# Laying out both members of 28 key pairs with ScalarE, so that GpSimd multiplies them in place with two instructions a step

## The reference

```python
sim = k @ q_i                                   # one token i, one head
_, top_idx = jax.lax.top_k(masked(sim), 8)
for comb in COMBS:                              # 8 single keys, then 28 pairs
    idx = concat(i, top_idx[comb])
    K, V = k[idx], v[idx]
    gram = jnp.einsum('cnd,cmd->cnm', K, K)     # dot products of all members
    log_det = jnp.log(where(valid, det(gram), 1.0) + 1e-06)
    score = log_det / (s + 1)
    w = softmax(K @ q_i / HS ** 0.5)
    out_s = jnp.einsum('cn,cnd->cd', w, V)
probs = softmax(scores)
y = probs @ outs
```

## Time and profile before

| | before |
|---|---|
| median of 3 runs (lowest to highest) | 6936.29 us (6931.03 to 6949.35) |
| the profiled execution: its time, its span | 6937.07 us, 6935.4 us |
| busy in the span: PE, DVE, POOL, ACT | 5118.2, 4327.0, 3276.0, 2100.8 us |
| attention phase, a stretch of 2840 us: busy PE, DVE, POOL, ACT | 2373.11, 2538.28, 1990.13, 993.06 us |

### The profile page before, as it was taken

How to read it: one execution, slowest core, us unless ns; L and a number is a source line. 1 busy time by engine, 2 the same in 40 slices (tenths; PEclk the granted TensorE clock), 3 DMA queues, 4 the chain that set the end, 5 groups by cost and what they waited for, 6 DMA issues and landing times. The chain is left out here.

```text
span 6935.4 us, 140450 instructions
## 1 busy us (share of the span) xinstructions
PE 5118.2 (74%) x45364; PEld 3716.5 (54%) x45365; DVE 4327.0 (62%) x9002; ACT 2100.8 (30%) x6098; POOL 3276.0 (47%) x4341
## 2 busy tenths in 40 slices
PE   6776766978888888888888888443980997169990
PEld 2333333765555555556555665342860776169990
DVE  5777775227888898898999999722654233212223
ACT  3343333223333333333333333222210332223330
POOL 1222222115666776777776767425236000554447
PEclk8677776996666666666666666556995997579995
DMA  4000000002222222222222222202222002111113
GB/s 138 5 7 5 7 3 6 0 5 71 74 74 70 75 72 72 73 75 71 74 72 72 75 72 75 67 26 73 75 72 68 0 0 60 52 50 46 46 42 109
DMA packets 170739, 369.46 MB, mean 53 GB/s; under 512 B 35650, under 2 KB 100939, under 8 KB 169140
## 3 DMA queue, kind: packets, MB, share of 16 engines
q1 hardware_dynamic: 136404, 283.77, 12.2%
q0 software_dynamic: 33792, 78.69, 3.6%
HBM read 286.86 MB, written 75.50 MB: 52 GB/s over the span
## 5 line engine op out<-in xcount | busy, mean ns | idle before, releaser
L2334 POOL TENSOR_TENSOR l2a_prod<-l2a_keys 128x64 f32<-128x64 f32 (+1 forms) x2304 | 1115.6, 514 | 817.2 <-ACT l2a_norms L2224 808.2
L2679 PE MATMUL l2a_g<-l2a_feat,l2a_onehot 128*128 128x33 bf16 x27648 | 894.1, 187 | 29.9 <-issue 24.8
L2679 PEld LDWEIGHTS l2a_g<-l2a_feat,l2a_onehot 128*128 128x128 bf16 x27648 | 835.8, 103 | 89.5 <-issue 61.1
L2648 PE MATMUL l2a_s<-l2a_qkT 32*128 32x128 f32 (+1 forms) x1536 | 653.6, 518 | 48.3 <-issue 48.3
L1734 POOL TENSOR_TENSOR l_hc<-l_hs,l_bc 128x512 f32<-128x512 f32 x192 | 243.0, 1266 | 803.2 <-DVE l_hs L1808 799.7
L2554 DVE TENSOR_REDUCE l2a_dots<-l2a_prod 128x72 f32<-128x1152 f32 x384 | 517.0, 1346 | 154.3 <-POOL l2a_prod L2340 154.3
L2545 DVE TENSOR_SCALAR l2a_onehot<-l2a_spread,l2a_key_col 128x2048 bf16<-128x2048 bf16 x576 | 544.7, 972 | 52.0 <-PE l2a_g L2679 45.0
L1903 PE MATMUL l_y<-l_hc,l_selT 128*96 128x512 f32 x384 | 316.5, 920 | 287.9 <-POOL l_hc L1734 287.9
L2597 PE MATMUL l2a_a<-l2a_tT,l2a_wqk 96*96 96x256 f32 x1024 | 453.4, 622 | 0.7 <-ACT l2a_tT L2175 0.7
L2648 PEld LDWEIGHTS l2a_s<-l2a_qkT 32*128 32x128 f32 x1536 | 320.5, 259 | 224.6 <-issue 181.7
L440 POOL DMA_INDIRECT rows_in<-l3f_dispatch_xn,l3f_dispatch_at x128 | 122.8, 959 | 651.2 <-ACT l3f_dispatch_xn L416 612.5
(11 more groups left out here) (403 smaller groups left out, 11255.9 us busy)
## 6 DMA issues: line engine op xcount, KB each, us to landing
l2a_spread<-index_rows SPq DMA_DIRECT2D x384, 512.0 KB
rows_in<-main_zeros SPq DMA_DIRECT2D x1, 13824.0 KB, 59.4
l2f_xg<-rows_in SPq DMA_DIRECT2D x72, 192.0 KB, 2.4
rows_out<-l2f_ys POOLq DMA_DIRECT2D x72, 192.0 KB, 2.4
l3f_xg<-rows_in SPq DMA_DIRECT2D x72, 192.0 KB, 2.4
rows_out<-l3f_ys POOLq DMA_DIRECT2D x72, 192.0 KB, 2.4
l3f_w<-in_l3f_w SPq DMA_DIRECT2D x2, 4608.0 KB, 33.6
l_xT<-in_l_xT SPq DMA_DIRECT2D x16, 384.0 KB, 3.9
```

What stands on the lines that cost most here:

```text
L2334: nc.gpsimd.tensor_tensor(made[:, j, at:at + wide * wide, :].rearrange("p (b a) f -> p b a f", b=wide), key[:, lo:lo + wide, :].unsqueeze( ...
L2648: nc.tensor.matmul(o, qkT[rows, u, h // 3, t * P:(t + 1) * P], qkT[rows, u, 4 + h // 3, 0:nk], start=True, stop=False, skip_group_check=True)
L2679: ins = nc.tensor.matmul(g_ps[j][:, a * FEAT:(a + 1) * FEAT], onehot[:, s[2] % 2, kt, j * SLOTS + a, :], feat3[:, s[1], kt, piece, h, :], ...
```

## The change

`keys` (8 keys a head) and `prod` (36 products a head) go. `left` (36 members a head) and `right` (28) come, both in two buffers for alternate steps. ACT copies the 8 keys into `left[0:8]`, and then both members of the 28 pairs from PSUM with six more copies, which repeat keys by broadcast: `left[8:36]` and `right[0:28]`. POOL then multiplies `left[8:36]` by `right` in place with one instruction for both heads, and `left[0:8]` by the token's own key with another. It waits for both heads before the first of them. DVE reduces `left` where it reduced `prod`. ACT's wait before the first head is now for `dots_ready` of two steps before.

```diff
--- before.py
+++ after.py
@@ -2026,10 +2026,10 @@
         index_rows = nc.dram_tensor("index_rows", (2, 2 * SLOTS * P), BF16).ap()
         spread = m.sb("spread", [P, 2, 2 * SLOTS, P], BF16)
         onehot = m.sb("onehot", [P, 2, 2, 2 * SLOTS, P], BF16)
-        keys = m.sb("keys", [P, 2, 2, SLOTS, HS])
+        left = m.sb("left", [P, 2, 2, NCOMB, HS])
+        right = m.sb("right", [P, 2, 2, COMBS, HS])
         values = m.sb("values", [P, 2, 2, HEADS, SLOTS + 1, HS])
         norms = m.sb("norms", [P, 2, 2, HEADS, SLOTS])
-        prod = m.sb("prod", [P, 2, 2, NCOMB, HS])
         dots = m.sb("dots", [P, LANES, NCOMB])
         top = m.sb("top", [P, LANES, SLOTS])
         ex = m.sb("ex", [P, LANES, 2 * SLOTS + COMBS])
@@ -2216,10 +2216,22 @@
 
                     q, t, h = count_of(s), s[2] // PAIRS, first_head(s[2]) + 3 * j
                     if j == 0:
-                        act.wait_ge(S["prod_ready"], counted(q - 1) if not (isinstance(q, int) and q < 2) else 1)
+                        act.wait_ge(S["dots_ready"], counted(q - 1) if not (isinstance(q, int) and q < 2) else 1)
                     act.wait_ge(S["gathered"], counted(q * 2 + (j + 1)))
                     src = g_ps[j][:, 0:SLOTS * FEAT].rearrange("p (a f) -> p a f", a=SLOTS)
-                    nc.scalar.copy(keys[:, s[2] % 2, j, :, :], src[:, :, 0:HS])
+                    key, lo, hi = src[:, :, 0:HS], left[:, s[2] % 2, j, :, :], right[:, s[2] % 2, j, :, :]
+                    halves = key.rearrange("p (g k) f -> p g k f", g=2)
+                    nc.scalar.copy(lo[:, 0:SLOTS, :], key)
+                    nc.scalar.copy(lo[:, 8:12, :], key[:, 0:8:2, :])
+                    nc.scalar.copy(hi[:, 0:4, :], key[:, 1:8:2, :])
+                    nc.scalar.copy(lo[:, 12:20, :].rearrange("p (g b a) f -> p g b a f", g=2, b=2),
+                                   halves[:, :, 0:2, :].unsqueeze(2).broadcast_to([P, 2, 2, 2, HS]))
+                    nc.scalar.copy(hi[:, 4:12, :].rearrange("p (g b a) f -> p g b a f", g=2, b=2),
+                                   halves[:, :, 2:4, :].unsqueeze(3).broadcast_to([P, 2, 2, 2, HS]))
+                    nc.scalar.copy(lo[:, 20:36, :].rearrange("p (b a) f -> p b a f", b=4),
+                                   key[:, 0:4, :].unsqueeze(1).broadcast_to([P, 4, 4, HS]))
+                    nc.scalar.copy(hi[:, 12:28, :].rearrange("p (b a) f -> p b a f", b=4),
+                                   key[:, 4:8, :].unsqueeze(2).broadcast_to([P, 4, 4, HS]))
                     nc.scalar.copy(values[:, s[1], t, h, 0:SLOTS, :], src[:, :, HS:2 * HS])
                     nc.scalar.copy(norms[:, s[1], t, h, :], src[:, :, 2 * HS]).then_inc(S["kv_ready"], 1)
 
@@ -2325,21 +2337,16 @@
 
                 def products(s):
                     q, t, u = count_of(s), s[2] // PAIRS, s[1]
-                    pool.wait_ge(S["dots_ready"], counted(q - 1) if not (isinstance(q, int) and q < 2) else 1)
-                    made, h = prod[:, s[2] % 2, :, :, :], first_head(s[2])
-                    for j in range(2):
-                        pool.wait_ge(S["kv_ready"], counted(q * 2 + (j + 1)))
-                        key = keys[:, s[2] % 2, j, :, :]
-                        for at, lo, hi, wide in ((12, 0, 2, 2), (16, 4, 6, 2), (20, 0, 4, 4)):
-                            nc.gpsimd.tensor_tensor(
-                                made[:, j, at:at + wide * wide, :].rearrange("p (b a) f -> p b a f", b=wide),
-                                key[:, lo:lo + wide, :].unsqueeze(1).broadcast_to([P, wide, wide, HS]),
-                                key[:, hi:hi + wide, :].unsqueeze(2).broadcast_to([P, wide, wide, HS]), ALU.mult)
-                    both = keys[:, s[2] % 2, :, :, :]
-                    nc.gpsimd.tensor_tensor(made[:, :, 8:12, :], both[:, :, 0:8:2, :], both[:, :, 1:8:2, :], ALU.mult)
-                    nc.gpsimd.tensor_tensor(made[:, :, 0:8, :], both,
-                                            feat[:, u, t, h:h + 4:3, 0:HS].unsqueeze(2).broadcast_to([P, 2, SLOTS, HS]),
-                                            ALU.mult).then_inc(S["prod_ready"], 1)
+                    made, h = left[:, s[2] % 2, :, :, :], first_head(s[2])
+                    pool.wait_ge(S["kv_ready"], counted(q * 2 + 2))
+                    hi = right[:, s[2] % 2, :, :, :]
+                    nc.gpsimd.tensor_tensor(made[:, :, SLOTS:, :].rearrange("p j k f -> p j (k f)"),
+                                            made[:, :, SLOTS:, :].rearrange("p j k f -> p j (k f)"),
+                                            hi.rearrange("p j k f -> p j (k f)"), ALU.mult)
+                    ins = nc.gpsimd.tensor_tensor(
+                        made[:, :, 0:SLOTS, :], made[:, :, 0:SLOTS, :],
+                        feat[:, u, t, h:h + 4:3, 0:HS].unsqueeze(2).broadcast_to([P, 2, SLOTS, HS]), ALU.mult)
+                    ins.then_inc(S["prod_ready"], 1)
 
                 def body(n, u, i, back, last):
                     if back(3):
@@ -2551,7 +2558,7 @@
                         q, t = count_of(s), s[2] // PAIRS
                         dve.wait_ge(S["prod_ready"], counted(q + 1))
                         h = t * HEADS + first_head(s[2])
-                        nc.vector.tensor_reduce(dots[:, h:h + 4:3, :], prod[:, s[2] % 2, :, :, :], AX.X, ALU.add
+                        nc.vector.tensor_reduce(dots[:, h:h + 4:3, :], left[:, s[2] % 2, :, :, :], AX.X, ALU.add
                                                 ).then_inc(S["dots_ready"], 1)
                     for k, do in ((SIMS, sim_stage), (DENOM, denom_stage), (GAP, gap_stage), (DET, det_stage),
                                   (SCORE, score_stage), (ROWS, row_stage), (ALPHA, alpha_stage)):
```

## The result

The changed kernel takes 7174.11 us in the median of 4 runs (7170.55 to 7183.74), against 6937.27 us (4 runs, 6931.03 to 6949.35) before: 1.0341 times as long, with a 95% interval of 1.0323 to 1.0359, so 237 us more. The profiled execution took 7176.38 us, with a span of 7174.8 us.

What follows compares the result with a forecast made beforehand. VectorE was taken to bound the attention phase, busy 2538 of 2840 us and stopped by GpSimd at shared SBUF ports. Waits +2.4 and ports +7.1 us an image, x 32 = 304 us, gave 7240 us from 6937, range 7040 to 7420.

Steps and rivals of the forecast that it cites:

- the forecast: Attention phase: VectorE loses 2.4 us an image to waits and 7.1 to ports, 304 us in all; 55% chance.
- ScalarE's copies: ACT, each head: seven copies take 1.24 us for 0.16, 830 us over 384 steps; second head ready after 3.2 us.
- Rival 3: ACT becomes the chain: repeated-source copies don't overlap, 0.8 us more a head; 7445 us, 12% chance.
- The large multiply: POOL's 896-element instruction takes 1.9 us, bounds 1.6 to 2.2, by the nearest row of dense operands.
- A stopped instruction loses what is left of GpSimd's: SBUF ports: a blocked VectorE instruction loses all that is left of the POOL instruction, however long.
- Rival 1: Faster: VectorE's port loss follows the time POOL holds the ports, 11.3 to 6.5 us an image; 6860 us, 13% chance.
- Ports by body: VectorE's loss to the ports, summed over bodies 0 to 11: 18.4 us an image for 11.3, so +7.1.
- Rival 2: Half the size: in bodies 5 to 7 the large multiply falls on the next body's maxima; 7087 us, 17% chance.
- Waits: VectorE's dots waiting for later products, bodies 0, 2, 3 and 11: 6.9 us an image against 4.5, so +2.4.
- "TensorE gives nothing back": Attention phase: no time is regained from TensorE, which stands before the index in the phase's waits already.
- The signs: Profile after: onehot's mean near 1 us; veto's addition, scores' and gaps' instructions show single ones over 2 us.

Runs made afterwards that it cites:

- split7_pool_only: pool_only with its large multiply in seven pieces of 128 elements, pair products still left out of the result: 6965.47 us, 1.0052.
- pool_only: The changed kernel without ScalarE's six further copies a head; pair members are ones, so scores are left out of the result: 7148.31 us, 1.0329.
- split7: The changed kernel with its 896-element GpSimd multiply in seven pieces of 128, copies and wait for both heads kept: 7166.34 us, 1.0353.
- headwise: The changed kernel with its large multiply in two of 448 elements, each waiting for its own head: 7091.81 us, 1.0245.
- dots_late: The kernel before, with VectorE's dots of bodies 0 and 1 moved behind their stage: 6933.43 us, 1.0014.
- split4: The changed kernel with its large multiply in four pieces of 224 elements, both heads waited for first: 7165.88 us, 1.0346.

## Why the prediction was right

It said 7240 us, within 7040 to 7420, by the forecast with most of the chance. It came out slower, by that mechanism, at 78% of the size (237 for 304 us).

- **ScalarE's copies.** Said 1.24 us from the first start of a head to the values' copy: 3538.57 to 3539.77 is 1.20. Said the second head is ready 3.2 us after the first start: 3541.50 + 0.23 - 3538.57 = 3.16. The 1.5 us that the prediction gives beside it, as an estimate, were too long. Rival 3 (copies that don't overlap, 0.8 us more a head) is out, and its price was too high: seven times the 0.264 us that it goes by is 1.85, so 0.6 above 1.24. A head has 1.04 us more than before, not 1.08, so 799 us by starts; busy time rose by 766, not 830.
- **The large multiply.** Said 1.9 us, with bounds of 1.6 and 2.2. It takes 2.07, 2.31 ns an element. I went by the nearest row, 792 elements in 1.68 (2.12 each); the row of 512 in 1.26 (2.46 each) erred by less the other way.
- **A stopped instruction loses what is left of GpSimd's.** This held: 2.12 us for an instruction of 0.207 beside one of 2.07. Rival 1 (the loss follows the time that the ports are held) is refuted twice. GpSimd is busy for 496 us less and the loss grew by 6.4 us an image; and split7_pool_only loses half as much as pool_only, although seven pieces of 0.442 us (3.1) stand there for one of 2.07. The point from which rival 1 was to decide, a second head ready less than 3 us into the body, wasn't reached in body 4, which began at 3537.32 (4.4 us before).
- **Ports by body.** Said 18.4 in all, measured 17.7. Bodies 3 to 7 were said to be 2.2, 2.4, 1.4, 2.3, 2.2 and came out at 2.2, 2.5, 1.5, 2.0, 2.3. Off were body 0 (2.7 said, 2.1 measured), body 2 (0.8, 1.2), body 9 (0.1, 0.6) and body 11 (2.0 said, 0.9 measured). Two were too small by 0.9 us and two too large by 1.7, so the sum is better than its parts. Rival 2, which took the loss from bodies 5 to 7, did not come.
- **Waits.** Said +2.4 us an image, measured +3.5: the term was too small. Body 3 was said to be 2.5 and came to 2.9. I had given body 11 0.7 and body 1 nothing; they have 1.7 and 1.4. Body 0, said to be 3.0, has 1.5 in the mean: the one image that I read waited longer there than most do (before 1.92, where the mean of 30 images is 1.56). These errors partly cancelled.
- **"TensorE gives nothing back".** This sentence was wrong. Against my 9.5 us an image the ports were 0.7 less and the waits 1.1 more; the 1.25 given back and the 0.9 that the account leaves between its sum and the image are what brought it to 7.8. Before, VectorE sat idle for 44.8 us in front of the onehots, waiting for TensorE (45.0 over the whole span); after, the whole wait in that group is 15.7, 8.0 of it for the DMA. Part of the time that VectorE now loses at the ports and before the dots, it had lost there already. Other idle time shrank by 1.25 us an image, 40 us in all.
- **The signs.** The onehots' mean was said to stay near 1 us: 0.996, for 0.976. The veto's addition was to show single ones of over 2 us; it didn't (0.608 at most), because the large multiply begins only as it ends. The scores' subtraction (L2472, up to 2.461) and the gaps' product (L2490) do show them:

```profile
L2490 DVE TENSOR_TENSOR l2a_gap<-l2a_det,l2a_ex x32: 857/2610/2621, 1711.4 to 4708.2; 128x672 f32<-128x672 f32 x32
```

My theory of what to mend failed where the prediction did not. I took ports and waits for two costs that could be removed one after the other, and split7, headwise and dots_late each showed that the removal of one raises the other.

## What to carry to other kernels

Where GpSimd and VectorE both read SBUF, count for each GpSimd instruction what VectorE runs beside it, and not GpSimd's busy time: a merge of eight multiplies into two, with less work in all, cost 3.3% without any added copy, and the same elements in pieces of 128 cost 0.5%. Before a cost at the ports is moved, look where the work lands next: a product that ends later turns port time into waits, and a consumer that comes later turns waits into port time. When the waits of one engine grow, take off what it already spent waiting for others.

## What the runs showed of the hardware

- **A GpSimd multiply can be kept from the ports by instructions that follow one another closely, and need not be.** In headwise it begins a few ns after the first of the four minors' instructions in both patterns, at 3389.09 and at 3482.72. In the one GpSimd takes 1.23 us, little above its shortest, and the second instruction stands still. In the other the four and the veto's addition all keep their shortest times, the multiply ends 2.55 us after it began, and the first VectorE instruction to be held is the one at 3484.32, behind a pause of 0.04 us. I found nothing in the timeline ahead of the two that differs, and no run settles what decides. The Trainium skill ("SBUF — State Buffer", section "SBUF: two separate sides") has the pair go to whoever starts first, for the whole instruction. The trace agrees for a single instruction; the row of 2.55 us shows that a GpSimd instruction that waits isn't always next.
- **The loss is the GpSimd instruction less some 0.15 us**, when that begins 0.06 us ahead: VectorE's took 2.12 us for 0.21 at its shortest, a loss of 1.91 beside 2.07.
- **Length and fixed cost of the dense in-place multiply.** Shortest times were 0.646 us for 224 elements (split4), 1.118 for 448 and 2.068 for 896. The two steps give 2.11 and 2.12 ns an element, with 0.17 us fixed; 128 elements by that are 0.44, and split7 shows 0.442. So seven pieces cost 1.0 us more than one, which is half of what the products of split7 took longer in the body shown; the rest is likely time at the ports. The Trainium skill ("GPSIMD Engine Reference", section "3.1 Elementwise — side-by-side cycle accounting") has some 2.6 cycles of 1.2 GHz an element for two inputs, by which one element takes 2.17 ns (an estimate from that page); the slope here is 2% below it.

The shortest times are the first number behind the count, in single lines of the source of split4, split7 and headwise:

```profile
L2345 POOL TENSOR_TENSOR l2a_left<-l2a_left,l2a_right x1536: 646/661/1480, 1604.6 to 4671.7; 128x224 f32<-128x224 f32 x192
```

```profile
L2345 POOL TENSOR_TENSOR l2a_left<-l2a_left,l2a_right x2688: 442/454/1272, 1610.9 to 4680.7; 128x128 f32<-128x128 f32 x192
```

```profile
L2344 POOL TENSOR_TENSOR l2a_left<-l2a_left,l2a_right x768: 1118/1137/2555, 1597.8 to 4603.8; 128x448 f32<-128x448 f32 x192
```

The longest of headwise, 2555, is the piece of body 4 above.
